# First group of a cross-attention and feed-forward kernel: V projected in one go of 154 columns, Wk in four transfers, and a new order on all queues

## The reference

```python
# layernorm (no affine) of x, cross attention with one head, residual
n = layernorm(x)
Q, K, V = n @ Wq + bq, ctx @ Wk + bk, ctx @ Wv + bv      # all 512 wide
s = where(mask, Q @ K.T / sqrt(512), -1e9)               # per batch, 2048 x 77
x = x + softmax(s) @ V @ Wo + bo
# feed-forward with cos and sin of weights plus noise
n = layernorm(x)
re, im = n @ cos(theta + theta_noise), n @ sin(phi + phi_noise)
x = x + sqrt(re * re + im * im)
```

## Time and profile before

| what | value |
|---|---|
| three runs | 246.16, 246.94 and 250.35 us, median 246.94 |
| the profiled execution's own time | 245.63 us |
| its span | 243.8 us |
| PE busy | 236.7 us, 97% of the span |
| first matmul of the feed-forward | at 44.01 us |
| first matmul of group 1's feed-forward | at 69.47 us |
| granted clock of PE | 0.996 over the span |

### The profile page before, as it was taken

The page is one execution under the profiler, slowest core; times in us unless marked ns, Lnnn a source line. Parts: engine busy times, 40 slices in busy tenths (PEclk is TensorE's granted clock), DMA queues, the critical chain, the costliest instruction groups (busy, mean ns, idle before and its releaser), DMA issues.

```text
span 243.8 us, 3987 instructions
## 1 busy us (share of the span) xinstructions
PE 236.7 (97%) x1283; PEld 138.8 (57%) x1283; DVE 169.4 (69%) x339; ACT 146.8 (60%) x256; POOL 52.0 (21%) x154
## 2 busy tenths in 40 slices
PE   8999999999999999999999999999999999999992
PEld 2898656448544584458544854476447644444472
DVE  1674999897886966787668775877587753873443
ACT  2213398991498357944695378646873589266433
POOL 1002057210520332023302330033104310132000
PEclk9999999999999999999999999999999999999998
DMA  6999987965239825872487257744874326413622
GB/s 183 389 427 415 413 237 127 266 205 104 46 65 279 343 48 184 168 297 87 108 208 266 108 126 218 215 173 94 224 241 175 69 60 89 172 43 86 212 88 91
DMA packets 48525, 44.80 MB, mean 184 GB/s; under 512 B 42518, under 2 KB 42774, under 8 KB 45309
## 3 DMA queue, kind: packets, MB, share of 16 engines
q1 hardware_dynamic: 47557, 43.37, 57.5%
q0 software_dynamic: 288, 1.05, 2.6%
q10 hardware_dynamic: 664, 0.18, 0.3%
HBM read 25.66 MB, written 8.39 MB: 140 GB/s over the span
## 4 chain that ended last, share of the span: by engine, by line
PE 76%; DMA 8%; ACT 6%; DVE 5%; issue 2%; POOL 1%; SPq 1%; POOLq 0%; DVEq 0%; ACTq 0%
PE re L486 8%; PE re L488 7%; PE re L487 7%; PE im L486 7%; PE im L488 7%; PE im L487 7%; PE score_bank L536 7%; DMA wqT<-in_WqT 3%; DMA hT<-h_split 3%; PE att L464 2%; PE att L462 2%; DMA out_rows<-wv 2%; PE re L549 2%; PE im L549 2%; PE re L553 2%
## 5 line engine op out<-in xcount | busy, mean ns | idle before, releaser
L761 ACT ACTIVATE h<-x,shift,rstd 128x512 f32<-128x512 f32 x28 | 22.7, 809 | 32.9 <-POOL shift L369 32.8
L536 PEld LDWEIGHTS score_bank<-a_keys,xTb 128*128 128x128 f32 x192 | 35.9, 190 | 8.2
L486 PE MATMUL re<-w_hi,hT 128*128 128x512 f16 x100 | 37.9, 379 | 0.3 <-DMA hT<-h_split 0.3
L486 PE MATMUL im<-w_hi,hT 128*128 128x512 f16 x100 | 37.9, 379 | 0.0
L488 PE MATMUL re<-w_hi,hT 128*128 128x512 f16 x100 | 37.9, 379 | 0.0
L488 PE MATMUL im<-w_hi,hT 128*128 128x512 f16 x100 | 37.9, 379 | 0.0
L487 PE MATMUL re<-w_lo,hT 128*128 128x512 f16 x100 | 37.9, 379 | 0.0
L487 PE MATMUL im<-w_lo,hT 128*128 128x512 f16 x100 | 37.9, 379 | 0.0
L1042 DVE SCALAR_TENSOR_TENSOR h_split<-h,h_split 128x512 f16<-128x512 f32 x32 | 22.1, 691 | 21.2 <-ACT h_split L765 20.8
L536 PE MATMUL score_bank<-a_keys,xTb 128*128 128x77 f32 x192 | 32.8, 252 | 0.0
L780 ACT ACTIVATE sq_re<-re 128x512 f32<-128x512 f32 x27 | 15.8, 587 | 18.6 <-PE re L488 14.6
(11 more groups left out here) (178 smaller groups left out, 425.8 us busy)
## 6 DMA issues: line engine op xcount, KB each, us to landing
xTb<-in_xT SPq DMA_DIRECT2D x8, 1024.0 KB, 4.9
xb<-in_x SPq DMA_DIRECT2D x8, 1024.0 KB, 5.7
out_rows<-wv SPq DMA_DIRECT2D x7, 1024.0 KB, 4.2
wk<-in_Wk SPq DMA_DIRECT2D x2, 512.0 KB, 5.5
wqT<-in_WqT SPq DMA_DIRECT2D x4, 256.0 KB, 7.4
wv<-in_Wv SPq DMA_DIRECT2D x1, 1024.0 KB, 12.8
wo<-in_Wo SPq DMA_DIRECT2D x1, 1024.0 KB, 15.6
angle_w<-in_theta SPq DMA_DIRECT2D x2, 512.0 KB, 18.7
```

The source lines that it names most:

```text
L486: nc.tensor.matmul(bank_[:, :], hT[j][:, 0, k, :], w_hi[part][:, k, :], start=(k == 0), stop=False)
L536: last = nc.tensor.matmul(score_bank[:, KEYS * j:KEYS * j + KEYS], xTb[:, k, P * j:P * j + P], a_keys[:, k, KEYS * batch:KEYS * batch + KEYS],
L761: nc.scalar.activation(h[j % 2][:, :], x2[b][:, j, :], ACT.Identity, bias=shift2[:, j:j + 1], scale=rstd2[:, j:j + 1]).then_inc(h_made, 1)
```

## The change

V is projected for both batches at once, 154 columns, four times four matmuls. Wk comes in four transfers and ctxT in two, and PE multiplies K chunk by chunk over all four banks. The second x tile (batch 1) and theta with its noise come in quarters, one semaphore each, interleaved. The transposed probabilities are copied before the Sin table is loaded and after the first theta pass; the norm's matmul moves ahead of the last `attend_first`; GpSimd issues the second noise DMA before the second tile's reciprocal root; DVE, ACT, PE and SP work in new orders. In the diff, lines that are only "..." stand for what is left out (semaphores, renamed waits, the later part of the ACT and DVE queues).

```diff
+            def load_theta(c):
+                cols_ = slice(DIM * c, DIM * c + DIM)
+                sp.dma_start(angle_w[0][:, cols_], theta[:, cols_]).then_inc(ld_theta[c], 16)
+                sp.dma_start(angle_n[0][:, cols_], theta_noise[:, cols_]).then_inc(ld_theta[c], 16)
...
+            def load_second_x(j):
+                sp.dma_start(xb[1][:, j, :], x[1, 0, :, j, :]).then_inc(ld_second_x[j], 16)
+
             for half in range(2):
                 chunks = slice(CH // 2 * half, CH // 2 * half + CH // 2)
-                sp.dma_start(wk[:, chunks, :], Wk[:, chunks, :]).then_inc(ld_wk[half], 16)
+                sp.dma_start(ctx_t[:, chunks, :], ctxT[:, chunks, :]).then_inc(ld_ctx[half], 16)
+                for k in range(CH // 2 * half, CH // 2 * half + CH // 2):
+                    sp.dma_start(wk[:, k, :], Wk[:, k, :]).then_inc(ld_wk[k], 16)
             for k in range(CH):
                 sp.dma_start(wqT[:, k, :], WqT[:, k, :]).then_inc(ld_wq[k], 16)
             load_xT(0, 0)
             load_x(0, 0)
             sp.dma_start(wv[:, :, :], Wv).then_inc(ld_wv, 16)
             sp.dma_start(wo[:, :, :], Wo).then_inc(ld_wo, 16)
-            load_x(1, 0)
-            load_angles(0, 0)
-            load_angles(0, 1)
-            load_angles(1, 0)
+            load_second_x(0)
+            load_second_x(1)
+            load_theta(0)
+            load_theta(1)
+            load_second_x(2)
+            load_second_x(3)
+            load_theta(2)
+            load_theta(3)
+            load_phi(0)
             sp.wait_ge(scores_mm, 1)
             load_xT(1, 0)
-            load_angles(1, 1)
+            load_phi(1)
 
             def transpose_h(m, tiles):
...
-            transpose_h(0, [0, 1])
+            transpose_h(0, [0])
+            transpose_h(0, [1])
             sp.wait_ge(scores_mm, 2)
             load_xT(0, 1)
+            sp.wait_ge(vw_hi_ready, 1)
+            sp.dma_start(vw_stack[1][REST - KEYS:REST, :, :],
+                         vw_stack[0][0:KEYS, :, :]).then_inc(vw_stacked, 16)
             transpose_h(0, [2])
             sp.wait_ge(x2_made, TILES)
             load_x(0, 1)
-            sp.wait_ge(vw_hi_ready, 1)
-            sp.dma_start(vw_stack[1][REST - KEYS:REST, :, :],
...
             rstd_first(0)
+            add_noise(1)
             rstd_first(1)
-            add_noise(1)
-            rstd_of_x(1)
...
+            rstd_of_x(1)
...
-                                     start=(k == 0), stop=False)
-            pe.wait_ge(ld_wk[1], 16)
-            for c in range(CH):
-                for k in range(CH // 2, CH):
+            for k in range(CH):
+                if k % (CH // 2) == 0:
+                    pe.wait_ge(ld_ctx[k // (CH // 2)], 16)
+                pe.wait_ge(ld_wk[k], 16)
+                for c in range(CH):
                     last = nc.tensor.matmul(prep[c][:, 0:KK], wk[:, k, P * c:P * c + P], ctx_t[:, k, :],
-                                            start=False, stop=(k == CH - 1))
-                last.then_inc(kT_mm, 1)
+                                            start=(k == 0), stop=(k == CH - 1))
+                    if k == CH - 1:
+                        last.then_inc(kT_mm, 1)
 
             for k in range(CH):
...
-                    last = nc.tensor.matmul(bank_[:, cols_], wv[:, k, P * c:P * c + P], ctx_t[:, k, cols_],
+                    last = nc.tensor.matmul(bank_[:, 0:KK], wv[:, k, P * c:P * c + P], ctx_t[:, k, :],
                                             start=(k == 0), stop=(k == CH - 1))
                 last.then_inc(vT_mm, 1)
 
             def project_values(b, k):
...
-            pe.wait_ge(a_ready, CH)
-            scores(0, 0)
-            pe.wait_ge(ld_wv, 16)
-            values_of(0, 0)
-            values_of(0, 1)
-            pe.wait_ge(ld_wo, 16)
-            pe.wait_ge(c_ready, 1)
-            project_values(0, 0)
-            values_of(0, 2)
-            project_values(0, 1)
-            values_of(0, 3)
-            project_values(0, 2)
...
-            project_values(0, 3)
-            values_of(1, 2)
-            values_of(1, 3)
-            pe.wait_ge(vw_ready, 1)
-            pe.wait_ge(pT_copied, 1)
-            pe.wait_ge(vT_ready, CH + 1)
-            attend_first(0)
-            project_values(1, 2)
-            values_of(1, 0)
-            pe.wait_ge(vT_ready, CH + 2)
-            attend_first(1)
-            project_values(1, 3)
-            values_of(1, 1)
-            project_values(1, 0)
-            attend_first(2)
-            pe.wait_ge(ld_bo, 16)
-            project_values(1, 1)
-            scores(1, 1)
-            attend_first(3)
...
+            pe.wait_ge(a_ready, CH)
+            scores(0, 0)
+            pe.wait_ge(ld_wv, 16)
+            values_of(0)
+            values_of(1)
+            values_of(2)
+            pe.wait_ge(ld_wo, 16)
+            pe.wait_ge(c_ready, 1)
+            project_values(0, 0)
+            values_of(3)
+            project_values(0, 1)
+            pe.wait_ge(consts_made, 2)
+            pe.wait_ge(probs_made, 1)
+            for j in range(TILES):
+                last = nc.tensor.transpose(pT_bank[0:KEYS, P * j:P * j + P], probs[:, j, :], ident[:, :])
+            last.then_inc(pT_mm, 1)
+            project_values(0, 2)
+            project_values(0, 3)
+            pe.wait_ge(pT_copied, 1)
+            project_values(1, 0)
+            pe.wait_ge(vw_ready, 1)
+            pe.wait_ge(pT_copied, 1)
+            attend_first(0)
+            project_values(1, 1)
+            attend_first(1)
+            project_values(1, 2)
+            attend_first(2)
+            pe.wait_ge(ld_bo, 16)
+            project_values(1, 3)
+            scores(1, 1)
+            pe.wait_ge(key_norm_made, 1)
+            nc.tensor.matmul(pT_bank[:, 0:1], ones_keys[:, :], key_norm[:, :], start=True, stop=True).then_inc(vw_norm_mm, 1)
+            attend_first(3)
             feed_first(0, 0, 0)
             feed_first(0, 0, 1)
-            pe.wait_ge(key_norm_made, 1)
-            nc.tensor.matmul(pT_bank[:, 0:1], ones_keys[:, :], key_norm[:, :], start=True, stop=True).then_inc(vw_norm_mm, 1)
             feed_first(1, 0, 0)
             feed_first(1, 0, 1)
             feed_first(0, 1, 0)
+            imag_and_score(1, 0, 0)
+            feed_first(0, 1, 1)
             feed_first(2, 0, 0)
-            feed_first(0, 1, 1)
             feed_first(2, 0, 1)
-            imag_and_score(1, 0, 0)
-            imag_and_score(1, 1, CH)
+            imag_and_score(1, 1, 4)
             pe.wait_ge(vw_stacked, 3 * 16)
...
-            values_turned(0, 0)
-            values_turned(0, 1)
+            values_turned(0)
             exps(0)
-            values_turned(0, 2)
-            values_turned(0, 3)
+            values_turned(1)
+            values_turned(2)
+            values_turned(3)
+            act.wait_ge(quarter_made, 1)
+            turns_of(0, 0)
             act.wait_ge(pT_mm, 1)
             nc.scalar.activation(probsT[:, :], pT_bank[0:KEYS, :], ACT.Copy).then_inc(pT_copied, 1)
-            values_turned(1, 2)
-            values_turned(1, 3)
-            act.wait_ge(quarter_made, 1)
-            turns_of(0, 0)
-            turns_of(0, 1)
-            values_turned(1, 0)
             nc.scalar.activation(act_scratch[:, 1:2], zero[:, :], ACT.Sin)
             sine(0, 0)
+            turns_of(0, 1)
             high_half_of_sine(0, 0)
+            sine(0, 1)
             high_first(0)
-            values_turned(1, 1)
-            sine(0, 1)
-            turns_of(1, 0)
+            high_half_of_sine(0, 1)
             act.wait_ge(vw_mm, 2)
             nc.scalar.activation(vw[:, 1, :], pT_bank[0:KEYS, :], ACT.Copy).then_inc(vw_ready, 1)
+            turns_of(1, 0)
             high_first(1)
             act.wait_ge(vw_ready, 2)
             nc.scalar.activation(vw_squares[:, :, :], vw[:, :, :], ACT.Square, accum_out=key_norm[:, :]).then_inc(key_norm_made, 1)
-            high_half_of_sine(0, 1)
+            sine(1, 0)
+            high_half_of_sine(1, 0)
             turns_of(1, 1)
-            sine(1, 0)
...
-            stats_of_x(0, 0)
+            stats_of_x(0, 0, [0])
+            stats_of_x(0, 0, [1])
+            stats_of_x(0, 0, [2])
+            stats_of_x(0, 0, [3])
...
-            softmax_shift(0, 0)
-            stats_of_x(1, 0)
-            softmax_total(0)
-            sum_angle(0, 0)
-            dve.wait_ge(ld_bo, 16)
-            values_ready()
+            logits_of(0, 0)
+            top_of(0)
+            stats_of_second_x(0)
+            sum_theta(0)
+            stats_of_second_x(1)
+            sum_theta(1)
+            stats_of_second_x(2)
+            stats_of_second_x(3)
+            reduce_angle(0, 0)
             dve.wait_ge(stats1_made, 2)
             mean_of_x(1)
-            sum_angle(0, 1)
+            dve.wait_ge(ld_bo, 16)
+            dve.wait_ge(vw_mm, 1)
```

(27 more changed lines are left out.)

120 lines of the change are left out of this document (53 added, 67 removed).

## The result

The changed kernel takes 253.94 us (median; 253.0 to 255.4), the kernel before 247.02 in the same runs: 1.0317 times the time, 95% interval 1.0284 to 1.0349. I had forecast 245.7, 243.8 to 248.2. The forecast was wrong, in its sign too.

What follows compares the result with a forecast made beforehand. PE's own work, busy 97% of the span, was taken as the bound. Feed-forward start 1.06 us earlier, net +0.16 behind it, gave -0.84 and 244.8; shifted to the median of four, 245.7 us, range 243.8 to 248.2.

Steps and rivals of the forecast that it cites:

- From there both programs are the same.: From group 1 on, nothing differs, so the gain at group 1, 0.84 us, is the whole gain.
- the sum: Whole program: feed-forward start gains 1.06 us, net +0.16 behind it, so -0.84 at group 1: 244.8 against the profiled execution.
- my rivals: Whole program: all keeps up 244.95 (22%), hT later 247.7 (18%), clock falls 250.0 (4%), small pieces slow 251.3 (3%).
- The clock: At the feed-forward's start, a wait for hT reaching 2.5 us halves the clock; with the wait +3.4 us, 250.0; 4%.
- Loads: Smaller transfers ahead of the feed-forward: 0.35 us later for everything behind Wq, phi 1.2 us later.
- PE's path: Preparation on PE: 2.76 us of V work and the 0.55 us vT wait removed; PE's own work ends at 42.2.
- wait for `vw[0]`: Before the first attend_first, PE waits 0.95 us for DVE, until 30.6.
- The start of the feed-forward: First feed-forward matmul at 42.95 against 44.01, set by hT and w_lo, a gain of 1.06 us.
- the two limits I had worked out: At the feed-forward's start: hT landing at 42.9 behind the second noise DMA, and DVE's w_lo at 42.9.
- My chain for it: DVE ahead of the feed-forward: from rstd_first(1) ending at 38.6, steps of 4.3 us in all make w_lo at 42.9.
- Cutting PE's path alone: Ahead of the feed-forward, less PE work by itself gains only 0.3 us, as hT's path ends 0.3 us apart.

Runs made afterwards that it cites:

- the tail put back: Changed kernel with DVE's calls at the end of group 0 in the order of the kernel before: 247.1 us, 1.0037 times the kernel before.
- the one with the fillers: Changed kernel, DVE's end of group 0, Wk and ctxT transfers as before, five warm-up matmuls ahead of the norm's matmul: 246.57 us, 1.0000.
- The version without fillers: Changed kernel with DVE's end of group 0, Wk and ctxT transfers as before, no warm-up matmuls added: 246.97 us, 1.0042.
- with fillers: Kernel before with only V projected in one go, plus 13 warm-up matmuls in PE's wait for hT: 247.16 us, 1.0017.
- 18 fillers: Changed kernel with 18 warm-up matmuls in PE's wait ahead of group 1's first attention matmul: 251.1 us, 1.0189.

## Why the prediction was wrong

**The step that failed** is "From there both programs are the same." It ended the sum at group 1, on the ground that the loops are unchanged. The feed-forward matmuls are, but the diff of DVE's queue runs on until `step(1, 1, 1)`, and six of its lines there change what SyncE's queue waits for during group 1. The rule that the forecast states for DVE's 20 to 43 us (a reordering there delays something) it didn't apply 25 us later. Undone alone, this order gives back 6.8 us; put alone into the kernel before, it costs 3.6, and the rest of its price there is made by the low clock and the later preparation. None of my rivals had it. The row to read was in the trace of before: ACT's `p_split` at 72.06, with the residual at 69.63 ahead of it and at 74 behind it, SyncE's load at 71.05.

**The clock.** I named the mechanism (a wait, then matmuls at half speed) and priced it well (2.6 us forecast for one product of 12 matmuls, 2.9 measured for 14). Its condition was wrong. I let it begin at 2.5 us of idle time, read off the end of the program. In the change it followed 0.95 us at 42.2. So I put 4% on something that happened twice in one execution.

**Loads.** Taken 0.35 us behind Wq, measured 1.8. Wk lies in the first 6.7 us, which average 201 GB/s; I priced its pieces with the 370 of a later stretch, in which the queue was already full. The Trainium skill (DMA: Bandwidth & Descriptors, Rules for kernel authors) asks for large transfers, and for the start of the queue the two runs with Wk in halves again (16.5 against 18.5 in the change) bear it out in sign, with transfers of 512 KB against 256 KB and none of 1 MiB. Phi's halves landed at 32.5 and 36.2 (forecast 31.8 and 35.5).

**PE's path.** V merge 1.05 us per eight instructions, right; wait for `vw[0]` short instead of 0.95, since the scores' delay took it in (`attend_first(0)` at 31.12, forecast 30.6); norm 0.95 instead of 0.4, behind the first noise DMA. PE reached the last `attend_first` at 42.48, forecast 41.2.

**The start of the feed-forward**: 43.76, forecast 42.95, before 44.01. Of the two limits I had worked out, `w_lo` decided, at 43.6 instead of 42.9. My chain for it had no wait for ACT's turns of phi. There DVE stood 0.92 us, since the first noise DMA landed at 39.54 and not at 37.8: it left 0.9 later, behind phi, and took 6.7 us instead of 5.9. hT was there at 43.16 (42.9 forecast), 1.06 behind the noise instead of 1.35. That it hangs on the second noise DMA is shown by moving that DMA alone. The sum has a slip, too: 1.06 less 0.16 is 0.90, not 0.84. The versions with the tail put back and Wk in two start at 42.4 to 42.7 and reach group 1 at 68.6 to 69.0, where I had it (68.6); that they hit it is in part luck, since the first waits 0.59 for ACT's square at 48.36, where I had 0.16. The profiled execution of the one with the fillers has the gain: 244.86 us against 245.63 of before, spans 242.9 and 243.8. Its median has not: the other executions lie between 245.20 and 247.56. The low clock isn't why, since all twelve have a granted clock of 0.996 to 1.00; what spreads them stays open, as only one has a trace. The version without fillers goes from 246.06 to 248.72 with 0.986 to 0.993 in ten of twelve executions, so the fillers did keep the clock up, worth about 1 us by the two ratios, whose intervals just touch.

**Cutting PE's path alone** "buys 0.3 us and then idle time": it bought none, and the idle time brought the low clock: group 1 3.0 us later in the profile, the time 1.5 higher by the ratio.

## What to carry to other kernels

Follow a reordered queue to its last changed line, and for each moved wait list what stands behind it on its own engine and in the queues that wait for that; a ready instruction behind one that waits is the first thing to look for. Work taken off the bounding engine is worth only what the next path leaves: find it first (here one DMA on another queue), and move it with the cut. Count a new idle gap of TensorE as its length plus the low clock that may follow.

## What the runs showed of the hardware

- The length of a gap didn't decide whether the clock fell. It fell behind 0.78, 0.95, 1.21 and 1.47 us of idle time ahead of the norm, 2.24 ahead of batch 1's first projection, 2.74 ahead of the first product, 3.86 in group 1. It held behind 0.54 and 0.70 ahead of the norm, 1.65 and 1.71 behind the first product, 1.92 ahead of it (with fillers), and 2.92 and 3.26 in group 1. Two kernels that are the same up to there had 0.66 us ahead of the norm and 0.39 ahead of the first product, and 0.70 and 0.37: it fell in the first (18 fillers) and held in the second (only the residual moved). What tells them apart stays open. At the full clock the 128x512 f16 matmuls are 0.216 us apart, at 0.50 they are 0.427, for 3 to 7 us at a time.
- Matmuls put into a wait kept the clock up over all executions in two pairs of kernels: granted clock 0.997 to 1.00 in twelve of twelve against 0.986 to 0.993 in six of six (V alone, with and without them), and 0.996 to 1.00 in twelve of twelve against 0.986 to 0.993 in ten of twelve (Wk as before, tail put back).
- 1 MB of Wk in four transfers instead of two, and ctxT in two, near the start of the program, moved the first use of Wq from 8.8 to 9.4 us to 10.2 to 11.0. The first use of bias_q, on another queue, went from 6.63 to 7.86 with the change, but with Wk in two again it was still at 7.84 and 7.87, so Wk's pieces are not its cause.
- One transposing DMA issued at 37.2 or 37.5 was there at 41.3 or at 44.3, as a 512 KB accumulating DMA had left at 34.7 or 37.2; in sixteen traces it landed 0.9 to 2.8 us behind that DMA, never ahead of it. Another, `pT`'s, landed 1.8 to 2.1 us behind the 1 MB load issued ahead of it on the same queue in fifteen of them.
